# The value projections of a 16-head attention move to another PSUM bank and to the other steps

## The reference, cut to what matters

```python
q = (emb @ Wq.T).reshape(B, SQ, 16, 64).transpose(0, 2, 1, 3)
k = (context @ Wk.T).reshape(B, SK, 16, 64).transpose(0, 2, 1, 3)
v = (context @ Wv.T).reshape(B, SK, 16, 64).transpose(0, 2, 1, 3)
q = _layernorm(q, qn_w, qn_b)
k = _layernorm(k, kn_w, kn_b)
attn = softmax(einsum('bhqd,bhkd->bhqk', q, k) / 8)
out = einsum('bhqk,bhkd->bhqd', attn, v)
x = x + tanh(g_xattn[1]) * (out.reshape(B, SQ, 1024) @ Wu.T + bu)
```

## Time and profile before

| | |
|---|---|
| median of three runs | 1493.91 us |
| the profiled execution, its own time | 1494.78 us |
| its span | 1493.0 us |
| TensorE busy over the span | 1282.6 us, 86% |
| VectorE | 877.8 us, 59% |
| ScalarE | 711.9 us, 48% |
| GpSimd | 277.8 us, 19% |
| the stage of the change, about | 169 to 458 us from the start of the span |

### The profile page before, as it was taken

One profiled execution on the slowest core, in us unless ns is written; L12 is line 12 of the kernel. 1 busy time (PEld: TensorE's weight loads), 2 busy tenths in 40 slices (PEclk: granted clock), 3 DMA queues, 4 the chain that ended last, 5 costly groups with the idle time before them and its releaser, 6 DMA issues. The chain is left out here.

```text
span 1493.0 us, 26211 instructions
## 1 busy us (share of the span) xinstructions
PE 1282.6 (86%) x8587; PEld 958.4 (64%) x8587; DVE 877.8 (59%) x2280; ACT 711.9 (48%) x1529; POOL 277.8 (19%) x382
## 2 busy tenths in 40 slices
PE   6768489989987899779999979963999978999995
PEld 5742256666665487568888859852677764666664
DVE  4538788888873454556676643448687742222225
ACT  4323487777772302246666643432455533333333
POOL 1010032222231000023333330041443420000000
PEclk9869799999997999879999989965999978999998
DMA  9000000000000000000000022020000000000000
GB/s 349 2 1 0 1 1 1 2 1 2 2 1 1 1 1 0 1 1 2 2 2 2 2 59 70 1 113 1 1 2 0 0 1 0 0 1 1 0 1 29
DMA packets 6426, 24.48 MB, mean 16 GB/s; under 512 B 797, under 2 KB 1311, under 8 KB 5418
## 3 DMA queue, kind: packets, MB, share of 16 engines
q1 hardware_dynamic: 6314, 23.03, 4.5%
HBM read 21.98 MB, written 1.05 MB: 15 GB/s over the span
## 5 line engine op out<-in xcount | busy, mean ns | idle before, releaser
L1305 DVE SCALAR_TENSOR_TENSOR XN<-bank,gate,XN 128x128 f32<-128x128 f32 x256 | 89.9, 351 | 224.7 <-PE bank L1269 222.1
L1285 ACT ACTIVATE e_hidden<-bank,small 128x512 f32<-128x512 f32 x152 | 104.4, 687 | 214.8 <-PE bank L1257 214.7
L745 POOL TENSOR_TENSOR a_pn<-a_probs,a_rec 128x512 f32<-128x512 f32 x128 | 133.0, 1039 | 308.6 <-DVE a_rec L995 234.5
L1269 PEld LDWEIGHTS bank<-attention_weights,e_hidden 128*128 128x128 f32 x1024 | 119.2, 192 | 14.8 <-issue 14.8
L1009 DVE TENSOR_REDUCE a_mx<-bank 128x4 f32<-128x512 f32 x128 | 87.1, 681 | 70.2 <-PE bank L807 70.2
L1257 PE MATMUL bank<-XNT,attention_weights 128*128 128x512 f32 x256 | 121.2, 606 | 1.3 <-PEq L541 1.3
L1269 PE MATMUL bank<-attention_weights,e_hidden 128*128 128x128 f32 x1024 | 119.3, 275 | 0.0
L931 ACT ACTIVATE a_pT<-bank 128x512 f32<-128x512 f32 x128 | 76.1, 594 | 89.2 <-PE bank L842 89.0
L833 PE MATMUL bank<-attention_weights,a_cv 128*128 128x512 f32 x128 | 70.8, 635 | 27.3 <-issue 25.8
L1017 DVE TENSOR_TENSOR a_shifted<-bank,a_mx 128x512 f32<-128x512 f32 x128 | 88.3, 690 | 3.5
L990 DVE TENSOR_REDUCE a_total<-a_probs 128x4 f32<-128x512 f32 x128 | 86.5, 676 | 1.3 <-ACT a_probs L947 1.3
(11 more groups left out here) (351 smaller groups left out, 2584.9 us busy)
## 6 DMA issues: line engine op xcount, KB each, us to landing
attention_weights<-in_a SPq DMA_DIRECT2D x2, 2048.0 KB, 11.9
mod_ring<-in_mod_weights SPq DMA_DIRECT2D x4, 576.0 KB
ctx_both<-in_ctx SPq DMA_DIRECT2D x1, 2048.0 KB, 9.8
attention_weights<-in_up SPq DMA_DIRECT2D x1, 2048.0 KB, 7.9
attention_weights<-in_down SPq DMA_DIRECT2D x1, 2048.0 KB, 12.4
down<-in_down SPq DMA_DIRECT2D x1, 1536.0 KB, 18.3
down<-in_mod_weights SPq DMA_DIRECT2D x2, 576.0 KB
X<-in_x SPq DMA_DIRECT2D x4, 256.0 KB, 4.2
```

Source lines behind the costliest of these rows:

```text
L745: pool.tensor_tensor(pn[:, p, :].rearrange("p (h s) -> p h s", h=4), probs[:, p, :].rearrange("p (h s) -> p h s", h=4), rec[:, p, :].unsqu ...
L1269: last = pe.matmul(down_bank[j][:, 0:width], layer[0:rows, f, j * 128:(j + 1) * 128], down(g, f), start=f == 0, stop=f == NB - 1)
L1285: act.activation(hidden[0:rows, p, f, :], up_bank_of(i, f)[0:rows, :], function, bias=up_bias(g, f)).then_inc(hidden_ready, 1)
L1305: dve.scalar_tensor_tensor(out=total, in0=down_bank[j][:, e * D:(e + 1) * D], scalar=gate_column(k, 4 * q + j, g * per_group + e), in1=tot ...
```

## The change

Value projections write bank 4 in this stage, which `values` fills and `keep_o` empties, and do so with lag 8, in even steps. `project_v` now waits for `o_kept`, `values` for all the `v_kept` up to the step before. `turn_qk` has no wait for `v_kept` any more. `output` gets lag 14, `normalise` and `turn_x` lag 15, so that they stand in the step after. GpSimd's copy for the value projection is written at `at(3)` in place of `at(1)`: two steps later than before. The second call of the function, without `qk_norm`, keeps bank, lags and waits.

```diff
-        lag = {..., "project_v": 7, ..., "out": 13, "normalise": 14, "turn_x": 14}
+        lag = {..., "project_v": 8, ..., "out": 14, "normalise": 15, "turn_x": 15}
...
+        v_bank = value_bank if qk_norm is not None else qkt_bank
...
-                if at(1).alive and at(1).offset % 4 == 0:
-                    stage_v(batch_of(at(1)))
+                v_ahead = at(3 if qk_norm is not None else 1)
+                if v_ahead.alive and v_ahead.offset % 4 == 0:
+                    stage_v(batch_of(v_ahead))
...
-            def values(i):
+            def values(i, at):
-                await_count(pe, v_kept, m // 2 + 1)
+                await_count(pe, v_kept, (at(lag["project_v"] + 1).reached() + 1) // 2 if qk_norm is not None else m // 2 + 1)
...
             def turn_qk(i, at):
-                j = at(lag["project_v"])
-                if not j.before_first:
-                    await_count(pe, v_kept, (j.reached() + 1) // 2)
...
             def project_v(i, at):
                 if qk_norm is not None:
-                    j = at(lag["turn_qk"] + 1)
-                    await_count(pe, qk_kept, j.reached())
+                    j = at(lag["values"] + 1)
+                    if not j.before_first:
+                        await_count(pe, o_kept, j.reached() // 2)
-                pe.matmul(qkt_bank[:, :], cv[:, p, :], wv[:, g * 256:(g + 2) * 256], start=True,
+                pe.matmul(v_bank[:, :], cv[:, p, :], wv[:, g * 256:(g + 2) * 256], start=True,
...
             def keep_v(i):
-                               qkt_bank[:, :].rearrange("p (h w) -> p h w", h=8),
+                               v_bank[:, :].rearrange("p (h w) -> p h w", h=8),
```

More of the change, by code:

```diff
@@ L693, in stage_head_attention @@
     if qk_norm is not None:
-        lag = {"square": 1, "turn_qk": 2, "keep_qk": 3, "scores": 6, "project_v": 7, "subtract": 6, "exponentials": 7,
-               "sums": 7, "turn_p": 9, "keep_p": 9, "values": 12, "keep_o": 12, "out": 13, "normalise": 14, "turn_x": 14}
+        lag = {"square": 1, "turn_qk": 2, "keep_qk": 3, "scores": 6, "project_v": 8, "subtract": 6, "exponentials": 7,
+               "sums": 7, "turn_p": 9, "keep_p": 9, "values": 12, "keep_o": 12, "out": 14, "normalise": 15, "turn_x": 15}
     else:
@@ L868, in body @@
                 if at(lag["values"]).alive and at(lag["values"]).offset % 2 == 1:
-                    values(at(lag["values"]))
+                    values(at(lag["values"]), at)
                 if at(lag["project_v"]).alive and at(lag["project_v"]).offset % 2 == 0:
```

## The result

| | median | runs | ratio to before, 95% interval |
|---|---|---|---|
| before | 1493.61 us | 4 (1491.88 to 1495.25) | |
| changed | 1473.03 us | 4 (1472.22 to 1474.95) | 0.9864 [0.9847, 0.9881] |

The change is 20.6 us faster; 23.4 were forecast. The profiled execution of the changed kernel took 1472.67 us, 22.1 less than that of before, with a span of 1470.9.

The account below looks back on a forecast made before the run. A chain of hand-offs between engines, not one engine's work, was taken as the bound. Savings of 2.3 (start), 21.0 (steady part) and 0.1 (drain) sum to 23.4 us, giving a median of 1470.5 us, range 1467.5 to 1482.

Parts of the forecast that it names:

- Bank 6 as the cause of the stall: TensorE before the value projection: waits 1.23 us in step 1 and 0.46 in step 3 for keep_qk to free bank 6.
- TensorE's floor: TensorE's time per batch without the projection's idleness and lost overlap: 17.30 - 1.69 - 2 x 0.06 = 15.49 us.
- VectorE's at 15.55: VectorE's time per batch once four waits on TensorE and their lost overlap go: 17.30 - 1.75 = 15.55 us.
- the steady term: Steps 17 to 65, 12 batches: 1.75 us saved in each, 21.0 us in all.
- The start: Steps 9 to 16, before the first output: the same waits go in four rounds, 2.3 us saved.
- `keep_v` 1.1: Bank 4: ScalarE's copy of the projected values ends 1.1 us before the next values need the bank; cost 0.
- `keep_o` 0.85: Bank 4: ScalarE's copy, begun 2.56 us after values, ends 0.85 us before the next projection; cost 0.
- The transposition of X: turn_x, now in step 2: its input is ready 0.33 us before TensorE reaches it; cost 0, at worst 0.7 a batch.
- Half of it stays: VectorE's waits in steps 0 and 2 come from operation order; only 10.6 us saved, 1483 us; chance 12%.
- The norm hand-off takes over: TensorE stalls at turn_x waiting for VectorE as it did at the projection; no change, 1493 us; chance 6%.
- The ring: Bank 4's four uses in line hold up project_v behind keep_o and values behind keep_v; +16 us, 1510 us; chance 4%.
- the drain: End of the stage: a 1.60 us projection stall goes, batch 14's transposition waits 1.93 instead of 0.48; 0.1 us saved.

Follow-up runs that it names:

- e2: Changed kernel with output, normalise and turn_x kept at lags 13, 14, 14, so value projection's bank and step alone against before: 1473.59 us, ratio 0.9859.
- e3: Kernel before with only the lags of output, normalise and turn_x raised to 14, 15, 15; project_v stays in bank 6: 1493.32 us, ratio 0.9993.
- the new drain: Changed kernel with the transposition of X of batch 14 moved behind the last weighted values: 1467.14 and 1465.86 us, ratios 0.9821 and 0.9817 to before.

## Why the prediction was right

*Step by step.* Bank 6 as the cause of the stall: right, shown from both sides, by its removal and by the order of ScalarE's root. TensorE's floor was put at 15.49 and is 15.52; VectorE's at 15.55 and is at most 15.53. The period of 15.53 against 15.55 makes the steady term 21.2 against 21.0. The start was -2.29 against -2.3.

*The margins.* `keep_v` 1.1 forecast, 1.09 found. `keep_o` 0.85 forecast, over 1.6 found: the 2.56 that I took from step 1 of before held the very lateness that the change removes, and in step 3 it begins 1.79 after `values`. The transposition of X: 0.33 forecast, 0.11 found (301.15 against 301.26), since the head sums of step 2 come 0.84 us after `scores` and push the maxima; the margin was thin but TensorE never waited.

*The rivals.* Half of it stays: wrong, all four short waits of VectorE went. The norm hand-off takes over: wrong as a whole, but this is what limits e2 and e3, where the transposition of X waits 0.27 and 0.45 for VectorE. The ring: not binding in the steady part, but binding in the drain, with 0.83 us in three waits. The margin of 1.1 at `keep_v` was reckoned with the turnings and the query/key projection of a full step between, and the drain has no such projection.

*The term that was mis-sized* is the drain, -0.1 forecast and +2.63 measured. I had reckoned the uncovered wait of batch 14 (1.45) against the stall that goes (1.60), as separate sums. The wait did what was said, 1.94. But I priced the matmuls behind it at the full clock, because the earlier trace rows had shown a busier TensorE keeping it, and I never asked what a less busy one does. With 2.2 us for the clock added, the term is +2.1. The remaining 0.5 is about what the ring costs there: 0.83 before `values`, less a wait of 0.23 for `keep_v` before `turn_qk` that the kernel before had and the change removes. That is read off the profiles; no run isolates it.

## What to carry to other kernels

When an instruction waits in one engine's queue for a buffer that a second engine frees late because of a third, the sum of the gain is read from the floors of all three, not from the idle time of the first: here 1.69 us of TensorE's idleness and 1.75 of VectorE's chain named the same 1.77. A later lag helps the steady part and lengthens the drain; write out the drain's last ten instructions and price them with the clock that their own idle time leaves. Try the order of the waits before the buffers: one line moved in the kernel before gave half of this change, and one transposition moved in the changed kernel took 3.5 us more off the stage (6 by the medians, the difference being the open part behind the stage). Work out margins for the drain too: a buffer that is free in time in a full step need not be in a thin one.

## What the runs showed of the hardware

The granted clock fell from 2.4 to 1.2 GHz inside the drain of the changed kernel, around a wait of 1.94 us after the output of batch 14, and did not fall there in the new drain, with waits of 0.91 and 0.47 instead (425 to 430 us, granted 1.00). At the lower level 16 float32 products of 128 columns with their weights took 3.78 us instead of 2.05. Twelve idle-time transpositions (1.47 us) did not keep the clock over the 2.03 us between stages.
